# A decoder layer in one launch: queries and keys spread to head slots by DMA, running counts added by TensorE, scores scaled in four operations

## What is computed

```python
x = x + attention(layernorm(x))        # 16 heads of 8, rotary positions, causal mask, softmax
x = x + cross(layernorm(x), ctx)       # 16 heads, no softmax; ends in its own layernorm (gain ln_g, offset ln_b)
h = layernorm(x)                       # router and experts read this
expert = argmax(h @ centroids.T)       # one of 8 experts for each token
alpha  = sigmoid(h @ centroids.T)
x = x + out                            # out = alpha * (h + FFN_expert(norm(h))) + (1 - alpha) * h
```

## Time and profile before

| | us |
|---|---|
| median of 3 runs (lowest, highest) | 604.65 (603.29, 607.40) |
| the profiled execution's own time | 602.47 |
| its span, first to last instruction | 600.2 |
| mean granted TensorE clock | 0.989 of full speed |

### The profile page before, as it was taken

One profiled execution on the slowest core, in us unless ns is written; L12 is line 12 of the kernel. 1 busy time (PEld: TensorE's weight loads), 2 busy tenths in 40 slices (PEclk: granted clock), 3 DMA queues, 4 the chain that ended last, 5 costly groups with the idle time before them and its releaser, 6 DMA issues.

```text
span 600.2 us, 25006 instructions
## 1 busy us (share of the span) xinstructions
PE 528.8 (88%) x7951; PEld 410.0 (68%) x7951; DVE 496.4 (83%) x1762; ACT 492.7 (82%) x1358; POOL 421.1 (70%) x820
## 2 busy tenths in 40 slices
PE   2755999999999988999989999898879998999995
PEld 1533776666666666666666666666668898899994
DVE  3627899999999999999999999999768777777773
ACT  1735788988988888888888888888778797899993
POOL 1311568888888888888888888887757766555553
PEclk9996999999999999999999999999999999999999
DMA  5142112122122111232211211110301222322210
GB/s 150 41 57 52 29 35 63 43 58 55 56 78 88 57 55 56 66 92 63 56 56 57 59 52 39 38 38 22 86 21 56 70 64 72 98 74 67 68 53 14
DMA packets 55183, 35.35 MB, mean 59 GB/s; under 512 B 14977, under 2 KB 50434, under 8 KB 55057
## 3 DMA queue, kind: packets, MB, share of 16 engines
q1 hardware_dynamic: 50160, 24.44, 15.6%
q0 software_dynamic: 4320, 8.66, 4.3%
q10 hardware_dynamic: 576, 0.66, 0.4%
HBM read 24.46 MB, written 9.74 MB: 57 GB/s over the span
## 4 chain that ended last, share of the span: by engine, by line
POOL 31%; PE 29%; issue 22%; DVE 10%; ACT 2%; DMA 2%; DVEq 2%; POOLq 1%; SPq 0%; ACTq 0%
PE side L940 8%; POOL expert_rows L1980 6%; POOL pay L1952 4%; PE quad L925 4%; PE side L925 4%; POOL on L1900 3%; POOL rs_T L1914 3%; POOL x L1923 3%; POOL rs_L L1875 2%; DVE hT L1551 2%; PE side L661 1%; PE quad L909 1%; PE quad L690 1%; DMA mk<-in_mask 1%; POOL ve_L L1873 1%
## 5 line engine op out<-in xcount | busy, mean ns | idle before, releaser
L2013 POOL DMA_INDIRECT out<-yo,rb x71 | 70.1, 987 | 60.1 <-DVE yo L1757 53.8
L1980 POOL DMA_INDIRECT expert_rows<-pay,sli x64 | 65.5, 1024 | 33.9 <-DVE sli L1603 19.6
L1048 ACT ACTIVATE ex<-qk,cf 128x512 f32<-128x512 f32 x128 | 85.4, 721 | 0.1
L1409 DVE TENSOR_REDUCE mx<-quad 128x16 f32<-128x1024 f32 x64 | 77.5, 1219 | 4.5 <-PE quad L690 4.1
L940 PE MATMUL side<-w,hT 128*128 x568 | 76.8, 278 | 4.7 <-DVE hT L1551 3.1
L940 PEld LDWEIGHTS side<-w,hT 128*128 128x128 f32 x568 | 69.1, 192 | 7.6 <-issue 7.3
L1064 ACT ACTIVATE prob<-quad 128x1024 f32<-128x1024 f32 x64 | 65.8, 1032 | 3.0 <-PE quad L728 2.2
L1541 DVE TENSOR_SCALAR xh<-rb 128x128 f32<-128x128 f32 x71 | 25.2, 356 | 28.2 <-issue 23.3
L1088 ACT ACTIVATE xn<-x,mr,rs_T 128x128 f32<-128x128 f32 x64 | 28.1, 486 | 24.3 <-POOL mr L1916 24.1
L1161 ACT COPY w1b<-w 128x512 f32 x71 | 43.5, 615 | 0.3 <-issue 0.3
L1009 ACT ACTIVATE xn<-xin,rs_L 128x128 f32<-128x128 f32 x64 | 22.2, 394 | 24.8 <-POOL rs_L L1875 24.7
(11 more groups left out here) (270 smaller groups left out, 1634.1 us busy)
## 6 DMA issues: line engine op xcount, KB each, us to landing
rb<-expert_rows SPq DMA_DIRECT2D x71, 68.0 KB, 1.9
xin<-in_x SPq DMA_DIRECT2D x32, 128.0 KB, 3.3
cin<-in_ctx SPq DMA_DIRECT2D x32, 128.0 KB, 2.1
xr<-in_x SPq DMA_DIRECT2D x32, 128.0 KB
w<-in_w1t SPq DMA_DIRECT2D x8, 256.0 KB, 3.6
w<-in_w2t SPq DMA_DIRECT2D x8, 256.0 KB, 3.4
out<-yo,rb POOLq DMA_INDIRECT x71
expert_rows<-pay,sli POOLq DMA_INDIRECT x64, 2.9
```

The source lines that it names most:

```text
L1048: act(ex[g.par][:, i, :, :].rearrange("p a t -> p (a t)"), qk[g.par][:, :, :].rearrange("p a t -> p (a t)"), ACT.Copy, scale=own4[:, i:i + ...
L1409: v.tensor_reduce(mx[g.par][:, 2 * h_:2 * h_ + 2, :], quad[:, 2 * h_:2 * h_ + 2, :].rearrange("p r (h k) -> p r h k", k=SQ), AX.X, ALU.max ...
L1980: v.indirect_dma_start(out=rows, out_offset=bass.IndirectOffsetOnAxis(ap=sli[g.par][:, j:j + 1], axis=0), in_=pay[g.par][:, j, :], in_offs ...
L2013: v.indirect_dma_start(out=o_rows, out_offset=bass.IndirectOffsetOnAxis(ap=number, axis=0), in_=yo[b.c % 4][:, :], in_offset=None, bounds_ ...
```

## The change

- `ex` is no longer made by ACT. Queries and keys are laid out with the four heads of each strip of 32 interleaved (partition 4m+i of a strip is feature m of head i): the centred weights are written in that order (`WQP`, `WKP`, in three DVE operations instead of one), the exchange of halves becomes a shuffle by 16, and rotation tables and bias columns are loaded in that order. SP's new `by_head` issues four SBUF to SBUF DMAs for a group, each of 32 partitions with 2 KB each (64 KB), first in its round for group i-2, after a wait for POOL's `qk` of that group. The other parts of `ex` are cleared once, by a memset of 128x2048 on DVE and one on POOL. PE and POOL wait for these DMAs where they waited for ACT's copies.
- ACT issues 12 DMAs before its first round instead of 4.
- `place` is gone. PE `ranks` gets one more matmul in fp32: the identity times `cnt`, 24 columns, added in PSUM. `counted` copies `cnt` from PSUM. `own_rank` multiplies PSUM by the marks; it and `counted` change places.
- `scaled_scores` was one `tensor_tensor` over 128x48 into `tm`; it is four `tensor_scalar` operations over 128x8 each, in place in `y1`, with the scale read from `sc` as a pointer. `affinities` reads `y1`.

```diff
@@ SP
+            def by_head(g):
+                first(sp, g, s_clear, 2)
+                wait(sp, pe_s, g.n - 2, "s3")
+                wait(sp, pe_a, g.n - 2, "s3")
+                wait(sp, po_f, g.n, "qk")
+                for i in range(4):
+                    sp.dma_start(ex[g.par][i:P:4, i, :, :], qk[g.par][i:P:4, :, :]).then_inc(d_by[g.par], 16)
             def one(g):
+                stage(g, 2, by_head)
                 stage(g, 0, load_x)
@@ PE max_scores and scores
-                wait(pe, ac_f, g.n, "x3")
+                wait_dma(pe, d_by, g, 4)
@@ PE ranks
+                wait(pe, dv_r, g.n - 1, "tot")
+                mm(bank_[:, 0:(J + 1) * E].rearrange("p (a e) -> p a e", e=E), identf,
+                   cnt[:, :].unsqueeze(1).broadcast_to((P, J + 1, E)), start=True, stop=False)
@@ ACT
-                stage(g, 3, by_head, (2, 3))
...
-                stage(g, 2, by_head, (0, 1))
...
-            ac.dma_start(cf[:, 0:i0], consts[:, 0:i0]).then_inc(d_rope, 16)
-            ac.dma_start(bc[:, :], bcol).then_inc(d_rope, 16)
+            for r_ in range(4):
+                own = slice(32 * r_, 32 * r_ + 32)
+                ac.dma_start(cf[own, 0:4 * SQ], consts[own, 0:4 * SQ].rearrange("(i m) c -> m i c", i=4)
+                             ).then_inc(d_rope, 16)
+                ac.dma_start(bc[own, 0:4], bcol[own, 0:4].rearrange("(i m) c -> m i c", i=4)).then_inc(d_rope, 16)
+            ac.dma_start(cf[:, 4 * SQ:i0], consts[:, 4 * SQ:i0]).then_inc(d_rope, 16)
+            ac.dma_start(bc[:, 4:6], bcol[:, 4:6]).then_inc(d_rope, 16)
@@ DVE scaled_scores
-                v.tensor_tensor(tm[g.par][:, :, :, :],
-                                y1[g.par][:, :, D:D + 3 * E].rearrange("p j (a e) -> p j a e", e=E),
-                                sc[g.par][:, :, :].unsqueeze(3).broadcast_to((P, J, 3, E)), ALU.mult
-                                ).then_inc(*dv_r.done("ab"))
+                for j in range(J):
+                    for a in range(2):
+                        own = slice(D + a * E, D + (a + 1) * E)
+                        last = v.tensor_scalar(y1[g.par][:, j, own], y1[g.par][:, j, own], sc[g.par][:, j, a:a + 1],
+                                               None, ALU.mult)
+                last.then_inc(*dv_r.done("ab"))
@@ DVE place, counted, own_rank
-            def place(g):
...
-                v.tensor_tensor(cnt[:, :], cnt[:, :], at("ranks", g)[:, J * E:(J + 1) * E], ALU.add
-                                ).then_inc(*dv_r.done("tot"))
+                v.tensor_copy(cnt[:, :], at("ranks", g)[:, J * E:(J + 1) * E]).then_inc(*dv_r.done("tot"))
...
-                v.tensor_tensor(rk[g.par][:, :, :], rk[g.par][:, :, :], ohb[g.par][:, 0:J, :], ALU.mult
-                                ).then_inc(*dv_r.done("pr"))
+                v.tensor_tensor(rk[g.par][:, :, :], at("ranks", g)[:, 0:J * E].rearrange("p (j e) -> p j e", e=E),
+                                ohb[g.par][:, 0:J, :], ALU.mult).then_inc(*dv_r.done("pr"))
```

More of the change, by code:

```diff
@@ L174, in decoder_kernel @@
         ws = sb("ws", [P, 6, D])
-        WQ, WQR, WK, WKR, WV, WO = (ws[:, i, :] for i in range(6))
+        WQP, WKP, WV, WO = (ws[:, i, :] for i in (1, 3, 4, 5))
         wcx = sb("wcx", [P, 4 * D + E])
@@ L267, in decoder_kernel @@
         pay = two("pay", [P, J, ROW])
-        sc = two("sc", [P, J, 3])
-        tm = two("tm", [P, J, 3, E])
+        sc = two("sc", [P, J, 2])
         af = two("af", [P, J, E])
@@ L362, in decoder_kernel @@
         d_c = [sem(f"dma_ctx{i}") for i in range(2)]
+        d_by = [sem(f"dma_by_head{i}") for i in range(2)]
         d_s = [sem(f"dma_scatter{i}") for i in range(2)]
@@ L1039, in max_by_head @@
                 last.then_inc(*ac_s.done("x"))
[L1041 to L1050, removed]
             def max_high(g):
@@ L1400, in partners @@
                                  t2[g.par][:, :, :].rearrange("p a t -> p (a t)"),
-                                 [p ^ (HD // 2) for p in range(32)]).then_inc(*dv_f.done("sh"))
+                                 [p ^ 16 for p in range(32)]).then_inc(*dv_f.done("sh"))
                 if g.n == 1:
@@ L1465, in y_sum @@
                 first(dv, g, s_vec, 1)
-                wait(dv, dv_r, g.n - 2, "ab")
+                wait(dv, dv_r, g.n - 2, "af")
                 wait(dv, ac_t, g.n, "n")
@@ L1564, in alpha, with counted @@
                 v.reciprocal(pay[g.par][:, :, C_AL], ea1[g.par][:, :]).then_inc(*dv_r.done("al"))
-            def place(g):
-                wait(dv, dv_r, g.n - 1, "tot")
-                wait(dv, dv_r, g.n - 2, "sl")
+            def counted(g):
                 wait(dv, pe_r, g.n, "rank")
[L1571 to L1577, removed]
-                v.tensor_tensor(cnt[:, :], cnt[:, :], at("ranks", g)[:, J * E:(J + 1) * E], ALU.add
-                                ).then_inc(*dv_r.done("tot"))
+                v.tensor_copy(cnt[:, :], at("ranks", g)[:, J * E:(J + 1) * E]).then_inc(*dv_r.done("tot"))
                 if g.n == GT - 1:
@@ L1605, in one @@
             def one(g):
+                stage(g, 8, own_rank)
                 stage(g, 8, counted)
-                stage(g, 8, own_rank)
                 stage(g, 4, row_max, 0)
@@ L1789, in leftovers @@
                 if c == 8:
-                    place(g29)
+                    own_rank(g29)
                     counted(g29)
-                    own_rank(g29)
                 if c == 9:
@@ L1807, in leftovers @@
                 if c == 19:
-                    place(g30)
+                    own_rank(g30)
                     counted(g30)
-                    own_rank(g30)
                 if c == 20:
@@ L1823, in leftovers @@
                 if c == 25:
-                    place(g31)
+                    own_rank(g31)
                     counted(g31)
-                    own_rank(g31)
                     wait(dv, dv_r, g31.n, "tot")
@@ L1841, in _ @@
             rows_in(Block(2))
+            own_rank(g28)
             counted(g28)
@@ L1879, in rotated @@
             def rotated(g):
-                wait(po, ac_f, g.n - 2, "x3")
+                wait_dma(po, d_by, g.back(2), 4)
                 wait(po, pe_s, g.n - 2, "s3")
@@ L2001, in _ @@
             v.memset(mean_m[:, :], 1.0 / D)
-            for k in range(2):
-                v.memset(sc[k][:, :, 2], 1.0)
             v.memset(ones_b[:, :], 1.0).then_inc(s_pool, 1)
+            v.memset(ex[1][:, :, :, :], 0.0).then_inc(s_clear, 1)
             po.wait_ge(s_pool, 1)
```

35 lines of the change are left out of this document (18 added, 17 removed).

## The result

The changed kernel takes **620.43 us** (median of 4 runs, 618.41 to 621.25) beside 604.06 us (603.29 to 607.40) for the kernel before. The ratio is 1.0252, 95% interval 1.0219 to 1.0284: slower by 2.5%. Forecast were 615.7 us and 1.8%.

What follows compares the result with a forecast made beforehand. POOL was taken to set the period. 8.6 + 0.7 - 1.0 + 2.0 + 0.7 = +11.0 us on 602.47 gave 613.5, as a median 615.7 us; range 602 to 626.

Steps and rivals of the forecast that it cites:

- the signs that it named: Trace signs of being right, such as even rounds of 12.9 to 13.1 us and the mask's issue 2 to 3 us later.
- So POOL waits only about 0.15 us of 12.63 and sets the period.: Even rounds: POOL runs nearly without gaps, so only a later sli can move the period of 12.63 us.
- rival (a): Even rounds: scaled scores aren't held and finish early, POOL's wait goes, -3.6 us, total 601.3, as a median 603.4; chance 0.20.
- Both kinds of operation are thus held until POOL's instruction is done.: DVE's sli and xh, and the new tensor_scalar operations too, wait for POOL's running instruction through the shared port pair.
- Four operations for one: Scaled scores on DVE: sli and the scatter later by 0.36 us (-0.15 to +0.9), 24 even rounds, +8.6 us.
- Ranks and counts: DVE saves 0.46 us a round, worth 0 in even rounds; matmuls and small steps among the expert blocks, +0.7 us.
- Copies taken from ACT: 2.9 us a round leave ACT: 0 in even rounds, -1.0 us (0 to -7) before 113 us, where PE leads.
- The DMAs hidden: SP's by_head transfers land before PE asks, and x behind them fits by 0.9 us; cost 0.
- Rival (c): Even rounds: x lands late behind the by_head issues and DVE waits, +12 us on top, 628; chance 0.11.
- The start: Before the first round: ACT issues 8 more DMAs ahead of its table load, xn starts later; +2.0 us.
- The mask: Round 4: the mask's issue on SP stands behind four DMA issues and a wait for qk; +0.7 us (0.5 to 1.5).
- (b): PE-led rounds: freed ACT time lets exp and max_scores start 1.4 us earlier, -9.8 us, as a median 594.1; chance 0.11.

Runs made afterwards that it cites:

- experiment 8: Kernel before with slot numbers computed ahead of alpha, and the negated mean moved from POOL to ACT; ratio 1.0029.
- experiment 12: Changed kernel with one multiplication back, slot numbers first, rope and bias in four loads, and the negated mean moved from POOL to ACT; ratio 0.9827, 595.13 us.
- Experiment 4: Kernel before with the slot numbers (sli) computed ahead of alpha and tm on DVE; ratio 0.9903.
- experiment 2: Kernel before with the four tensor_scalar operations alone in place of the one multiplication; ratio 1.0219.
- experiment 3: Kernel before with the edit of ranks and counts alone; ratio 1.0003.
- experiment 10: Kernel before with slot numbers ahead of alpha and the edit of ranks and counts added; ratio 0.9925.
- experiment 1: Changed kernel with the scaled scores as one tensor_tensor over 128x48 again; ratio 1.0079.
- experiment 11: Changed kernel with one multiplication back, slot numbers ahead of alpha, and rope and bias in four loads, keeping transfers and ranks; ratio 0.9928.
- experiment 9: Kernel before with slot numbers ahead of alpha, run again as a yardstick for the third set; ratio 0.9900.

## Why the prediction was right, and where it was short

It forecast slower by 11.0 us on the profiled execution; it came to 16.3 by the spans and 16.4 by the medians. The sign, the place and the mechanism held; it was short by 5.3 us, by 1.9 in the start, 1.1 in four rounds that it didn't count, 1.0 that ACT's copies didn't give back, 1.1 at the end and 0.4 at the mask. Of the signs that it named, one was clearly off: the mask's issue came 4.8 us later, not 2 to 3; 3.9 of that is the start. By its own steps:

**"So POOL waits only about 0.15 us of 12.63 and sets the period."** The second half is right: the round follows POOL's chain in nearly every kernel above. In experiment 8 a wait for ACT lies in that chain, and in experiment 12 DVE or PE is as near a bound. The first half is wrong. It read the 0.68 us of one round as the time of issue, but those rows already say otherwise: `sli` ends at 152.65 and the scatter starts at 153.47, 0.82 us later, as in the earlier trace rows, so in that round too it waited for `sli`. Experiment 4 shows 0.53. The wait was 0.31 us. This didn't harm the forecast, since the change added to a wait that was there, but the bound of -0.15 and rival (a)'s 601.3 us rested on it, and a gain of 1% lay in the kernel before, unseen.

**"Both kinds of operation are thus held until POOL's instruction is done."** Right, and shown from both sides: `sli` takes 0.15 to 0.18 us free, 0.37 behind the rest of `on`, 0.87 and 1.28 behind `qk`, and ends 0.02 to 0.03 us after it. The rule of the Trainium skill that the prediction named (SBUF — State Buffer, the section on the two separate sides) agrees with these rows.

**Four operations for one, +0.36 us a round.** Measured +0.34 in the profile after, 0.37 in experiment 2. Taken alone and away from POOL they cost 0.58 against 0.16 us, about the same difference: behind a running `qk`, the first of them is hidden and three remain, as worked out. The 24 even rounds lost 8.60 us (311.65 against 303.05), to the tenth what was forecast; that it is so near is luck, since 0.36 was picked between 0.34 and 0.41. Where it was short is the count: the four rounds from group 3 to 7 lose too, 1.10 us together (54.19 against 53.09; with the one multiplication back it is 52.83, 1.36 less). That makes 9.7 us for 28 rounds.

**Ranks and counts, 0 in the even rounds and +0.7 at the end.** `own_rank` takes 0.114 us, `cnt` 0.153, so the 0.15 taken for both was good, and experiments 3 and 10 show that the saving is worth nothing. That `own_rank` fell from the 461 ns of the earlier trace rows is the same hold: it took 158 ns at the least with both operands in SBUF and 0.58 us beside `yg`, and takes 0.11 beside `yg` with one of them in PSUM. It also changed places with `counted`, but the rows of it beside `yg` in both kernels show that the place isn't the reason. The Trainium skill has this rule (SBUF — State Buffer, "Who interferes with whom"): a DVE instruction with at most one SBUF input and in no 2-port mode doesn't contend with GpSimd; the row agrees. The last stretch grew by 1.80 us, not 0.7. Six kernels with the rank edit (the changed one and experiments 1, 3, 10, 11, 12) lie between 184.3 and 185.9 us there, three without it (before, 4, 9) between 183.75 and 185.0, so a part may be this edit's and a part is what such a stretch varies by; experiment 2, without the edit, even has 188.0. How much, stays open.

**Copies taken from ACT, -1.0 us.** The step failed: next to nothing came back. With the four operations taken out again, the 28 rounds take 355.95 us beside 356.14, and the four before 113 us, in which PE leads, 52.83 beside 53.09; with experiments 10 and 11 it is 53.22 and 52.97. So 0.3 us at most, and PE's chain of the early rounds doesn't run through ACT's copies either.

**The DMAs hidden, 0.** Right. The four issues take 2.4 us in half of the even rounds and 2.8 to 3.7 in the others instead of 1.9, but x then lands in 2.4 instead of 3.3 us, and it is there in time, by 0.3 us in the round above and by 0.1 at the least rather than 0.9. Rival (c) didn't happen, but it was closer than forecast. Its price holds a slip: 1.2 less 0.8 is 0.4 and not 0.5 us, which gives some +9.6 us and 625 rather than 628. The estimate of 2.3 us, which the prediction set beside its sum, is from the Trainium skill's page DMA: Bandwidth & Descriptors (anatomy of one DMA); the page fits it to transfers that GpSimd issues, and these are issued by SP. The median of 2.4 us after the change lies near it, the 3.3 before doesn't.

**The start, +2.0 us.** This is the term that was mis-sized most, 3.86 us, above the upper bound of 3.4. The step "ACT issues 8 DMAs more, each about 0.48 us from start to start" took the price of plain loads and counted four strided ones. All eight are strided: 0.71 us from start to start each, the first 1.32, and the table load moved by 6.33. The bound used 0.72 for all eight and had no row for a first one.

**The mask, +0.7 us.** Measured 1.06. The SBUF to SBUF issues take 0.6 us each there instead of 0.47. But the same stretch is 39.9 us in some kernels with before's SP queue and 41.0 in others (experiments 8 and 9), so the size can't be told from its own variation.

**The rivals.** (a), four short operations that aren't held, fell with the first profile. (b), freed ACT time pays, was tested where it had its best chance, with POOL's wait gone, and gave nothing by itself (experiment 11 has 0.9928; experiment 10, which still copies with ACT, has 0.9925). It paid when POOL's work was moved there: the last experiment. (c) see above.

## What to carry to other kernels

If one engine sets the period, an operation on another engine is priced by when it ends relative to that engine, not by its length: an operation for which the two share a port should start before the other engine's long instruction, never just behind its start. Before shortening anything, look for the small result that the bounding engine waits for and compute it first; here moving one line gained 1%, and no part of the change, as it stood, gained anything. Freed time on an engine off the path was worth nothing here until work of the bounding engine was moved into it, at a place where nothing long stands ahead of it.

## What was not expected of the hardware

- An `issue` gap can hide a wait. Before the scatter it is 0.53 us where all inputs were long ready, and 0.77 in rounds in which `alpha` came 0.09 us after `qk`'s end. The time from the last input says more than the gap: 0.82 us after `sli` where that came last, 0.88 after `alpha`.
- Issue times on the DMA queues: 0.43 to 0.47 us for a plain load (0.58 for x in the changed kernel), 0.68 for one whose source is strided (1.30 for the first), 0.59 in the median for an SBUF to SBUF transfer of every fourth partition, single ones up to 1.93.
- One tensor_tensor of 48 numbers a partition took 0.16 us when it wasn't held. Most of its 0.82 in the kernel before was waiting, not work.
